# Merging the gated and the forward stage of a spectral convolution kernel, storing its modes once, and fetching the first weights earlier

## The chip, the cores and the metric

The kernel runs on one core of one Trainium2 chip. The metric is the time of one execution on the device in microseconds (us); lower is better. Five engines work side by side: PE (TensorE, matmuls), DVE (VectorE), ACT (ScalarE), POOL (GpSimd) and SP (SyncE, which only issues DMAs here). Each runs its own list of instructions in order, and they wait for each other on semaphores. 16 DMA engines move the data; SP, ACT and POOL each feed them through a queue of their own.

## The reference

`x` is 8 images of 64 channels of 256 x 256 pixels, float32, which is 134 MB. Two layers are computed, and each is added to its own input.

```python
# layer 0: x = x + L0(gn(x))
y   = einsum('bwhc,dc->bwhd', xp, mlp1_w) + mlp1_b      # C -> 3C
x1, x2 = shift1(y[..., :c]), shift2(y[..., c:2*c])      # one pixel in 4 directions
a   = sum(x1) + sum(x2)
bar = softmax(gelu(a @ sa1_w.T) @ sa2_w.T)              # 2 gates per channel
o   = (bar0 * x1 + bar1 * x2) @ mlp2_w.T + mlp2_b
o   = o * sigmoid(batchnorm(x) * wbn) * x
# layer 1: x = x + L1(gn(x))
x_ft = rfft2(x)
top  = einsum('bixy,ioxy->boxy', x_ft[:, :, :32, :32],  w1)   # complex
bot  = einsum('bixy,ioxy->boxy', x_ft[:, :, -32:, :32], w2)
out  = irfft2(top and bot in their corners, zero elsewhere)
```

`gn` is a group norm over pairs of channels. The four weight tensors of layer 1 (real and imaginary part of `w1` and `w2`, 64 x 64 x 32 x 32 each) are 16.8 MB each, 67 MB in all.

## The kernel before

The program has three blocks; at the end of a block all engines meet before the next one starts.

1. **Statistics.** SP loads `x` in tiles of 2 MB, DVE takes mean and variance of each (L288), and ACT adds up the edges that the shifts need.
2. **Gated stage** (layer 0). It has 128 steps, 32 for each pair of images. A step takes 8 rows of a pair: SP loads them (`mix_u`), POOL and ACT make a shifted copy (`mix_v`), PE convolves (L484), DVE gates the result in two passes (L752, then L759, which also adds up the pixels into `sums`), and ACT stores it to the scratch tensor `x_scratch` (L537). The block ends when all 128 stores have landed.
3. **Forward, mode and inverse stage** (layer 1), on one 192 KB area per partition named `arena`.

The **forward stage** reads the 8 images back as 64 tiles of 8 channels (2 MB each, two DMAs of 1 MB on SP's queue, L901). Each tile has 2 halves, so there are 128 halves, numbered `u`, 16 to an image. For each half DVE adds the two image halves (`sums_of`, L1255), POOL subtracts them (L1418), and PE transforms along rows (L985) and transposes (L999). DVE copies the turned blocks to `A` (`turned`, L1275). ACT squares the pixels for the variance (L1125). While an image runs through this, PE transforms the columns of the image before it in 5 parts (L1033), beside which the group norm's scale of that image is made. The scaled modes of a finished image are copied to `XB` by ACT and DVE (L1152, L1310). At `u % 16 == 11` DVE adds the mean to one mode (L1318) and writes the negated imaginary part to a third plane of `XB` (`negate`, L1314). ACT stores the modes to `modes_in` (L1160).

A complex product on real matmuls needs the modes of each image twice: as (real, imaginary) and as (-imaginary, real). Before, both copies are stored, 2 MB for an image, and both are loaded.

The **mode stage** has 8 chunks of 256 modes. A chunk needs 8 MB of weights, issued by POOL (`weights`, L1432, a real and an imaginary DMA of 4 MB), and 2 MB of modes, issued by SP (L920). There are two buffers for each. A chunk is two rounds `r` of matmuls (L1078); after each round ACT and DVE copy half of the result out (L1196, L1368) and ACT stores it to `modes_out`. `mixed` counts rounds. The buffers of chunk `ch` come free when chunk `ch - 2` is done:

```python
for ch in range(2, 2 * NCH):
    pool.wait_ge(mixed, 2 * (ch - 1))
    weights(ch, 0, C)
```

The first weights are issued by POOL behind all forward work, and the modes of the first chunks behind the stores of the last image.

The **inverse stage** turns the modes back into pixels: PE makes rows (L1094) and columns (L1104), DVE adds them to the tile of `x_scratch` (L1402), and POOL stores the tile to `out` (L1448), 2 MB each, 64 tiles in 8 buffers.

The order on each engine is the order of the code; there is no planner. In what follows `fwd_`, `mix_`, `mode_` and `inv_` at the start of a name say to which stage it belongs, and `B * NRF` (256) is the count of all row transforms.

## Time and profile before

| | before |
|---|---|
| median of 3 runs | 2747.92 us (2746.04 to 2749.49) |
| profiled execution, its own time | 2745.33 us |
| its span, first to last instruction | 2743.3 us |
| granted TensorE clock, mean | 0.957 |
| PE busy | 2146.6 us (78%) |
| DVE busy | 2021.8 us (74%) |
| ACT busy | 1404.3 us (51%) |
| POOL busy | 975.5 us (36%) |
| moved by DMA | 957.95 MB, mean 349 GB/s |

By time the stages are: statistics to about 340 us, gated stage to 1250, forward stage to 1810, mode stage to 2086, inverse stage to the end. A busy share is a mean over the whole span; which engine or transfer sets the end differs from stage to stage.

### The profile page before, as it was taken

What the parts mean: (1) busy time and instruction counts of PE and PEld (TensorE: products, weight loads), DVE (VectorE), ACT (ScalarE), POOL (GpSimd) and SP (SyncE); (2) the same over time, 40 slices, a digit from 0 to 9 for tenths busy, and PEclk for the clock granted to TensorE, in tenths of its full rate; (3) what the DMA queues carried; (4) which work ended last, traced back from release to release, by engine and by line L of the source; (5) the groups of instructions that cost most, each with busy time, mean ns of one, the idle gap of its engine ahead of it and who ended that gap; (6) DMA issues with size and microseconds to landing.
All of it is one profiled execution on the core that took longest, in us unless ns stands there. A gap on an engine that the chain in (4) does not pass through costs nothing.

```text
span 2743.3 us, 34783 instructions
## 1 busy us (share of the span) xinstructions
PE 2146.6 (78%) x12978; PEld 1066.9 (39%) x12978; DVE 2021.8 (74%) x2280; ACT 1404.3 (51%) x1757; POOL 975.5 (36%) x555
## 2 busy tenths in 40 slices
PE   0000099999999999996999999956777999888895
PEld 0000033333333333332555555536775555444452
DVE  8999989999999999997888888840003665555453
ACT  1111189888888888885777777720002221221110
POOL 1000035663456556546765656621000222111121
PEclk9999999999999999998999999988888999999997
DMA  9999789999999999988677777779998999999999
GB/s 400 431 431 421 325 273 353 340 342 342 344 340 350 329 344 354 338 278 331 251 272 274 276 274 270 253 261 332 397 400 333 409 417 417 417 417 417 417 417 379
DMA packets 420187, 957.95 MB, mean 349 GB/s; under 512 B 13996, under 2 KB 326108, under 8 KB 375932
## 3 DMA queue, kind: packets, MB, share of 16 engines
q1 hardware_dynamic: 230332, 594.31, 57.7%
q0 software_dynamic: 52208, 201.95, 18.5%
q10 hardware_dynamic: 137488, 159.53, 17.4%
q8 instruction: 104, 1.70, 0.2%
q14 instruction: 55, 0.45, 0.0%
HBM read 662.00 MB, written 293.60 MB: 348 GB/s over the span
## 4 chain that ended last, share of the span: by engine, by line
PE 29%; DMA 16%; DVE 5%; issue 2%; ACT 0%; SPq 0%; POOL 0%; ACTq 0%; DVEq 0%
DMA out<-arena 8%; PE psum L1104 8%; PE psum L985 7%; PE psum L1078 5%; PE psum L1033 4%; DMA arena<-modes_in 4%; PE psum L999 3%; DVE arena L1255 3%; DMA arena<-modes_out 2%; PE psum L1094 2%; DVE arena L1275 1%; DMA arena<-x_scratch 1%; DVE arena L1402 0%; DVE arena L1314 0%; DMA modes_in<-arena 0%
## 5 line engine op out<-in xcount | busy, mean ns | idle before, releaser
L484 PE MATMUL psum<-mix_u,wcur 128*64 128x512 f32 x2048 | 880.0, 592 | 2.1 <-DVE mix_u L588 2.1
L484 PE MATMUL psum<-mix_v,wcur 128*64 128x512 f32 x2048 | 880.0, 592 | 0.0
L1104 PE MATMUL psum<-tab_irow_icol,inv_t 128*128 128x512 f32 x1024 | 491.1, 603 | 48.9 <-ACT inv_t L1226 47.4
L484 PEld LDWEIGHTS psum<-mix_u,wcur 128*64 128x64 f32 x2048 | 278.0, 136 | 589.4 <-issue 581.5
L1402 DVE TENSOR_TENSOR arena<-arena,psum 128x1024 f32<-128x1024 f32 x256 | 312.5, 1221 | 225.6 <-PE psum L1104 220.1
L1418 POOL TENSOR_TENSOR arena<-arena 128x1024 f32<-128x1024 f32 x128 | 349.2, 2736 | 231.5 <-PE psum L985 185.8
L389 POOL COPY mix_v<-mix_u 64x2321 f32<-64x2321 f32 x126 | 383.8, 3046 | 13.8 <-PE psum L484 6.0
L752 DVE SCALAR_TENSOR_TENSOR tiles<-psum,pcur,tiles 128x2048 f32<-128x2048 f32 x128 | 300.6, 2349 | 49.9 <-PE psum L484 49.8
L759 DVE SCALAR_TENSOR_TENSOR tiles<-tiles 128x2048 f32<-128x2048 f32 x128 | 316.9, 2476 | 4.0
L530 ACT ACTIVATE tiles<-tiles,pcur 128x2048 f32<-128x2048 f32 x128 | 268.2, 2095 | 98.1 <-DVE tiles L759 94.3
L1448 POOL DMA_DIRECT2D out<-arena x128 | 115.3, 905 | 562.6 <-DVE arena L1402 562.6
L288 DVE BATCH_NORM_STATS2 stats<-tiles 128x6 f32<-128x512 f32 x512 | 305.3, 675 | 13.2 <-DMA tiles<-x 13.0
L1226 ACT ACTIVATE inv_t<-psum 128x256 f32<-128x256 f32 x256 | 97.5, 384 | 420.1 <-PE psum L1094 420.1
L985 PE MATMUL psum<-arena,tab_frow_fcol_both_ident 128*64 128x512 f32 x1024 | 262.5, 633 | 33.1 <-DVE arena L1255 33.0
L1125 ACT ACTIVATE arena<-arena 128x1024 f32<-128x1024 f32 x256 | 269.8, 1054 | 27.8 <-DMA arena<-x_scratch 25.4
L484 PEld LDWEIGHTS psum<-mix_v,wcur 128*64 128x64 f32 x2048 | 278.0, 136 | 0.0
L498 ACT ACTIVATE mix_v<-mix_u 64x2322 f32<-64x2322 f32 x128 | 273.8, 2139 | 6.1 <-POOL mix_u L380 3.0
L1104 PEld LDWEIGHTS psum<-tab_irow_icol,inv_t 128*128 128x128 f32 x1024 | 197.2, 193 | 191.8 <-issue 128.2
L1255 DVE TENSOR_TENSOR arena<-arena 128x1024 f32<-128x1024 f32 x128 | 254.7, 1991 | 2.8 <-DMA arena<-x_scratch 2.4
L518 ACT ACTIVATE tiles<-mix_u,pcur 128x2048 f32<-128x2048 f32 x128 | 254.5, 1988 | 0.1
L1078 PE MATMUL psum<-arena 128*16 128x64 f32 x4096 | 169.5, 355 | 89.1 <-issue 53.7
L403 PE MATMUL psum<-raw,s_ones_dmask_spread_npix 128*128 128x24 f32 x4 | 1.0, 385 | 297.7 <-PEq L211 297.7
(188 smaller groups left out, 2063.4 us busy)
## 6 DMA issues: line engine op xcount, KB each, us to landing
arena<-x_scratch SPq DMA_DIRECT2D x254, 1024.0 KB, 8.8
mix_u<-x SPq DMA_DIRECT2D x120, 1280.0 KB, 9.5
tiles<-x SPq DMA_DIRECT2D x64, 2048.0 KB, 12.4
x_scratch<-tiles ACTq DMA_DIRECT2D x128, 1024.0 KB, 8.9
out<-arena POOLq DMA_DIRECT2D x128, 1024.0 KB, 42.2
arena<-L_conv_w_real POOLq DMA_DIRECT2D x7, 4096.0 KB, 22.0
arena<-L_conv_w_imag POOLq DMA_DIRECT2D x7, 4096.0 KB, 31.4
arena<-modes_in SPq DMA_DIRECT2D x8, 2048.0 KB, 32.2
```

The source lines that it names most:

```text
L288: last = nc.vector.bn_stats(stats[:, at:at + 6], XT[t % NX][:, q * 512:(q + 1) * 512])
L389: nc.gpsimd.tensor_copy(V[n % NV][C:P, 0:k], U[n % NU][C:P, SHIFT:SHIFT + k]).then_inc(up_done, 1)
L484: last = nc.tensor.matmul(bank(k * 4 + q, 512, C, e * C), wcur[j][:, e, m * C:(m + 1) * C], taps[e][:, r0:r0 + 2, m:m + W], start=(m == 0) ...
L498: nc.scalar.activation(V[n % NV][0:C, 0:k], U[n % NU][C:P, 0:k], ACT.Copy).then_inc(low_done, 1)
L752: nc.vector.scalar_tensor_tensor(out=G[n % 4][:, :], in0=psum[:, k * SC:(k + 1) * SC], scalar=pcur[j][:, 3:4], in1=G[n % 4][:, :], op0=ALU ...
L759: nc.vector.scalar_tensor_tensor(out=G[n % 4][:, :], in0=G[n % 4][:, :], scalar=1.0, in1=XC[n % 4][:, :], op0=ALU.add, op1=ALU.mult, accum ...
L985: last = nc.tensor.matmul(bank(n % 4, 512, C, par * C), frow[:, par, :], ED[n // 2 % NE][par][:, n % 2 * 2:n % 2 * 2 + 2, :], start=True, ...
L1078: last = nc.tensor.matmul(psum[32 * k:32 * k + 2 * B, at:at + C], XM[j][:, :, kx * M2 + ky], WT[j][:, :, kw * M2 + ky], start=True, stop=True)
L1104: last = nc.tensor.matmul(bank(n % 2 * 2 + a), TS[n % 2][:, a * P:(a + 1) * P], icol, start=True, stop=True)
L1255: v.tensor_tensor(ED[h % NE][0][:, :, :], XWF[t % NXF][:, 0, half, :], XWF[t % NXF][:, 1, half, :], ALU.add).then_inc(sums_done, 1)
L1402: nc.vector.tensor_tensor(xw, xw, psum[:, n % 2 * 1024:n % 2 * 1024 + 1024] .rearrange("p (a k) -> p a k", a=2), ALU.add).then_inc(added, 1)
L1418: nc.gpsimd.tensor_tensor(ED[h % NE][1][:, :, :], XWF[t % NXF][:, 0, half, :], XWF[t % NXF][:, 1, half, :], ALU.subtract).then_inc(diff_do ...
```

## The change

- **One block and one area.** The gated and the forward stage stand in one block, so no engine meets the others between them. The gated stage's buffers lie in `arena` too. SP loads the first forward tiles where gated buffers come free: tile 0 after convolution 124 of 128, tile 1 after 127, tile 2 after 128, tile 3 when all stores have landed. The tables of the forward stage are loaded in the first block, those of the inverse stage at the end of the forward loads.
- **POOL makes the first two sums** as well as the first two differences, while DVE gates the last rows. The five small DVE operations on the group means move from ahead of the first sum to `u == 2`. There are 4 buffer pairs for sums and differences, not 3 (`NE`).
- **Modes once.** `XB` has two planes and `modes_in` one copy, 1 MB for an image; `negate` goes, and the signs sit in the table `fcol`. In the mode stage DVE makes the second copy of each chunk (`turn`): a shuffle that swaps neighbouring partitions, and a multiplication by a column of signs (`alt`). The loads of modes move from SP's queue to POOL's, each just ahead of the weights of its chunk.
- **First weights early.** POOL issues 50 of 64 output channels of chunk 0's weights ahead of its last subtraction, the other 14 at the end of the forward rows, and behind them 46 of 64 of chunk 1's. The last image's modes for chunk 0 go straight from `XB` to the chunk's buffer.
- **Inverse.** The first output tile is stored in four pieces, each after its own addition.

```diff
+            KB = 256
+            arena = sb(ph, "arena", [P, 192 * KB])
...
-                    for k in range(4):
-                        sp.wait_ge(stored[k], NI // 4 * 16)
...
                 @block.sync
                 def _(sp):
-                    for n in ("frow", "fcol", "both", "ident"):
-                        sp.dma_start(*TF[n]).then_inc(f_tab, 16)
                     for t in range(B * NG):
                         c, g = t // NG, t % NG * CG
+                        if t < NXF:
+                            sp.wait_ge(conv_done, NI - (4, 1, 0, 0)[t])
+                        if t % (2 * NG) == 0 or t == NXF - 1:
+                            for k in range(4):
+                                sp.wait_ge(x1_stored[k], ((c // 2 + 1) * NB if t != NXF - 1 else NI) // 4 * 16)
...
-                    for ch in range(2 * NCH):
...
-                        sp.dma_start(XM[j][:, :, :], xm[:, :, pos:pos + MC]).then_inc(w_loaded[j], 16)
...
-                    def negate(k0, k1):
-                        nc.vector.tensor_scalar(XB[:, 2, k0:k1, :], XB[:, 1, k0:k1, :], -1.0, None,
-                                                ALU.mult).then_inc(neg_done, 1)
...
+                    v.memset(onecol[:, :], 1.0)
+                    dve.wait_ge(o_done, NI)
+                    v.reduce_sum(sv[:, 0, 0:NQ], sums[:, :].rearrange("p (q n) -> p q n", q=NQ), axis=AX_X).then_inc(n2, 1)
...
+                    dve.wait_ge(sums_done, 2)
                     for u in range(NU_ + 1):
...
+                    def turn(j, b0, b1, n):
+                        to, of = XM[j][:, 2 * b0 + 1:2 * b1:2, :], XM[j][:, 2 * b0:2 * b1:2, :]
+                        v.stream_shuffle(to, of, [lane ^ 1 for lane in range(32)]).then_inc(x_turned, 1)
+                        dve.wait_ge(x_turned, n + 1)
+                        v.tensor_scalar(to, to, alt[:, 0:1], None, ALU.mult).then_inc(x_ready, 1)
+                    dve.wait_ge(x_loaded[0], 16)
+                    turn(0, 0, B - 1, 0)
+                    dve.wait_ge(first_moved, 32)
+                    turn(0, B - 1, B, 1)
                     for r in range(NRO):
...
+                        ch = r // 2 + 1
+                        if h == 0 and ch < 2 * NCH:
+                            dve.wait_ge(x_loaded[ch % 2], (ch // 2 + 1) * 16)
+                            turn(ch % 2, 0, B, ch + 1)
...
                 @block.gpsimd
                 def _(pool):
...
+                    pool.wait_ge(up_done, NI)
+                    pool.wait_ge(conv_done, NI - 3)
                     for h in range(2 * B * NG):
                         t = h // 2
+                        if h == 2 * B * NG - 1:
+                            pool.wait_ge(f_col_done, (B - 1) * PARTS)
...
+                            weights(0, 0, W0_EARLY)
...
+                        if h < 2:
+                            nc.gpsimd.tensor_tensor(ED[h][0][:, :, :], XWF[0][:, 0, half, :], XWF[0][:, 1, half, :],
+                                                    ALU.add).then_inc(sums_done, 1)
...
-                    weights(0, 0, C)
-                    weights(1, 0, C // 2)
-                    pool.wait_ge(modes_stored, B * 48)
-                    weights(1, C // 2, C)
+                    weights(0, W0_EARLY, C)
+                    pool.wait_ge(modes_stored, (B - 1) * 16)
+                    modes(0, B - 1)
+                    weights(1, 0, W1_EARLY)
+                    pool.wait_ge(f_col_done, B * PARTS)
+                    pool.wait_ge(modes_stored, B * 16)
+                    pool.wait_ge(first_moved, 32)
+                    modes(1, B)
+                    weights(1, W1_EARLY, C)
                     for ch in range(2, 2 * NCH):
                         pool.wait_ge(mixed, 2 * (ch - 1))
+                        modes(ch, B)
                         weights(ch, 0, C)
```

DVE between the gated and the forward stage, before. L752 and L759 are the two passes of the last gated step, L1255 the forward sums, L1263 and L1275 copies out of `psum`:

```order
L752 SCALAR_TENSOR_TENSOR tiles<-psum,pcur,tiles 128x2048
L759 SCALAR_TENSOR_TENSOR tiles,sums<-tiles 128x2048
L346 UNCONDITIONAL_BRANCH
L1230 UNCONDITIONAL_BRANCH
L1233 MEMSET fwd_ones 128x1
L1234 TENSOR_REDUCE norm_values<-sums 128x4
L1236 TENSOR_SCALAR norm_values<-norm_values 128x4
L1239 COPY norm_values<-psum 128x4 x2
L1240 TENSOR_SCALAR mrow<-psum 1x512
L1242 TENSOR_TENSOR norm_values<-norm_values 128x8
L1244 TENSOR_SCALAR norm_values<-norm_values 128x8
L1255 TENSOR_TENSOR arena<-arena 128x1024 x3
```

The same place now; L896 and L903 are the gated passes, L1264 the sums:

```order
L896 SCALAR_TENSOR_TENSOR arena<-psum,pcur,arena 128x2048
L903 SCALAR_TENSOR_TENSOR arena,sums<-arena 128x2048
L1254 UNCONDITIONAL_BRANCH
L1332 MEMSET fwd_ones 128x1
L1334 TENSOR_REDUCE norm_values<-sums 128x4
L1336 TENSOR_SCALAR norm_values<-norm_values 128x4
L1264 TENSOR_TENSOR arena<-arena 128x1024
L1272 COPY arena<-psum 128x512
L1284 COPY arena<-psum 128x2x68 x4
```

The block's end is gone, one sum stands where three stood, and the copies and the four groups behind them (L1239 to L1245) stand three sums later.

POOL at the end of the forward stage, before. L1418 is the subtraction, L1432 the weights; chunk 0 is the first 64x64x256 pair:

```order
L1418 TENSOR_TENSOR arena<-arena 128x1024 x128
L1432 DMA arena<-L_conv_w_real 64x64x256
L1432 DMA arena<-L_conv_w_imag 64x64x256
L1432 DMA arena<-L_conv_w_real 64x32x256
L1432 DMA arena<-L_conv_w_imag 64x32x256
```

The same place now; L1471 is the subtraction, L1447 the weights, L1485 the modes:

```order
L1471 TENSOR_TENSOR arena<-arena 128x1024 x126
L1447 DMA arena<-L_conv_w_real 64x50x256
L1447 DMA arena<-L_conv_w_imag 64x50x256
L1471 TENSOR_TENSOR arena<-arena 128x1024
L1447 DMA arena<-L_conv_w_real 64x14x256
L1447 DMA arena<-L_conv_w_imag 64x14x256
L1485 DMA arena<-modes_in 128x7x256
L1447 DMA arena<-L_conv_w_real 64x46x256
L1447 DMA arena<-L_conv_w_imag 64x46x256
L1485 DMA arena<-modes_in 128x8x256
```

Two weight DMAs stand ahead of the last subtraction, and the modes stand in the same queue as the weights.

DVE at the start of the mode stage now (before, the 16 copies L1368 follow each other). L1382 and L1384 are `turn`, L1395 is the copy of a round's result:

```order
L1382 STREAM_SHUFFLE arena<-arena 128x7x256
L1384 TENSOR_SCALAR arena<-arena,tab_frow_fcol_both_ident_alt 128x7x256
L1382 STREAM_SHUFFLE arena<-arena 128x256
L1384 TENSOR_SCALAR arena<-arena,tab_frow_fcol_both_ident_alt 128x256
L1395 COPY arena<-psum 128x1024
L1382 STREAM_SHUFFLE arena<-arena 128x8x256
L1384 TENSOR_SCALAR arena<-arena,tab_frow_fcol_both_ident_alt 128x8x256
```

From here on a shuffle and a multiplication of 2048 elements stand between the two copies of each chunk but the last.

## Rows read from the trace of the kernel before

**Rows 1.** The page's part 2: GB/s moved in 40 equal slices.

```profile
GB/s 400 431 431 421 325 273 353 340 342 342 344 340 350 329 344 354 338 278 331 251 272 274 276 274 270 253 261 332 397 400 333 409 417 417 417 417 417 417 417 379
```

**Rows 2.** The chain that ended last: start us, us, what.

```profile
1824.68 35.39 DMA arena<-modes_in
```

**Rows 3.** Timeline where the gated stage ends: start us, us, engine line op.

```profile
1240.75 0.59 PE L484 MATMUL psum<-mix_u,wcur 128*64 128x512 f32 x1
...
1246.00 0.08 DVE L759 DVE_READ_ACCUMULATOR tiles<-tiles 128x1 f32 x1
...
1250.92 0.29 DVE L1234 TENSOR_REDUCE norm_values<-sums 128x4 f32<-128x128 f32 x1
...
1258.32 0.67 DVE L1240 TENSOR_SCALAR mrow<-psum 1x512 f32<-1x512 f32 x1
...
1261.83 10.01 DVE L1255 TENSOR_TENSOR arena<-arena 128x1024 f32<-128x1024 f32 x3 [2.35 <-DMA arena<-x_scratch]
```

**Rows 4.** Groups of instructions by line, 1325 to 1800 us: busy us, mean ns.

```profile
L1318 DVE TENSOR_TENSOR arena<-arena,ncur 64x1 f32<-64x1 f32 x7 | 16.2, 2321 | 0.0
...
L1314 DVE TENSOR_SCALAR arena<-arena 64x2048 f32<-64x2048 f32 x7 | 8.5, 1208 | 0.0
```

**Rows 5.** Timeline of DVE in the forward stage, two images four apart.

```profile
1515.64 2.32 DVE L1318 TENSOR_TENSOR arena<-arena,ncur 64x1 f32<-64x1 f32 x1
1517.89 1.21 DVE L1314 TENSOR_SCALAR arena<-arena 64x2048 f32<-64x2048 f32 x1
...
1795.58 2.32 DVE L1318 TENSOR_TENSOR arena<-arena,ncur 64x1 f32<-64x1 f32 x1
```

**Rows 6.** Timeline of PE at the same place.

```profile
1522.45 3.56 PE L985 MATMUL psum<-arena,tab_frow_fcol_both_ident 128*64 128x512 f32 x8 [1.55 <-DVE arena L1255]
...
1526.97 1.94 PE L985 MATMUL psum<-arena,tab_frow_fcol_both_ident 128*64 128x512 f32 x8
```

**Rows 7.** Busy time by window there; after POOL: granted clock, DMA share, GB/s.

```profile
1522.40:1526.10 3.70, 3.65 (x9) 0.92 (x10) 2.66 (x7) 1.62 (x4) 0.00 (x0) 0.55 1.01 337
```

**Rows 8.** Timeline of POOL, end of the forward stage and mode stage.

```profile
1795.08 2.80 POOL L1418 TENSOR_TENSOR arena<-arena 128x1024 f32<-128x1024 f32 x1 [0.51 <-PE psum L985]
1809.15 1.71 POOL L1432 DMA_DIRECT2D arena<-L_conv_w_real  x1 [11.27 <-PE psum L999]
...
1881.55 1.82 POOL L1432 DMA_DIRECT2D arena<-L_conv_w_real  x1 [37.92 <-PE psum L1078]
```

**Rows 9.** Timeline of DVE at the end of the forward stage.

```profile
1802.54 1.20 DVE L1255 TENSOR_TENSOR arena<-arena 128x1024 f32<-128x1024 f32 x1
...
1824.12 2.08 DVE L1310 TENSOR_SCALAR arena<-psum,ncur 64x256 f32<-64x256 f32 x5 [5.30 <-PE psum L1033]
```

**Rows 10.** Timeline of PE in the mode stage.

```profile
1860.31 32.41 PE L1078 MATMUL psum<-arena 128*16 128x64 f32 x804 [35.21 <-DMA arena<-modes_in]
...
2060.91 11.92 PE L1078 MATMUL psum<-arena 128*16 128x64 f32 x283 [3.66 <-issue]
...
2079.52 4.16 PE L1078 MATMUL psum<-arena 128*16 128x64 f32 x101 [0.67 <-issue]
```

**Rows 11.** Busy time by window: end of the forward stage, mode stage.

```profile
1785.00:1810.00 25.00, 21.54 (x128) 11.55 (x127) 22.67 (x47) 15.91 (x31) 11.19 (x5) 1.00 0.40 85
...
1920.00:2000.00 80.00, 61.57 (x1468) 58.06 (x1460) 7.92 (x6) 7.08 (x6) 8.17 (x5) 0.90 1.03 397
```

**Rows 12.** The page's part 5 and part 6: a long DVE pass, and the loads of modes.

```profile
L759 DVE SCALAR_TENSOR_TENSOR tiles<-tiles 128x2048 f32<-128x2048 f32 x128 | 316.9, 2476 | 4.0
...
arena<-modes_in SPq DMA_DIRECT2D x8, 2048.0 KB, 32.2
```

**Rows 13.** Busy time by window in the inverse stage.

```profile
2108.00:2114.00 6.00, 6.00 (x18) 3.04 (x17) 3.22 (x4) 1.12 (x3) 1.79 (x2) 1.00 0.52 216
2114.00:2120.00 6.00, 6.00 (x18) 3.23 (x17) 3.77 (x4) 1.12 (x3) 0.21 (x1) 1.00 0.68 264
...
2200.00:2700.00 500.00, 451.63 (x1233) 237.40 (x1232) 273.69 (x233) 98.35 (x226) 91.92 (x103) 0.95 1.02 417
```

480 lines of the change are left out of this document (256 added, 224 removed).

## The prediction, made before the changed kernel was run

> **What bounds the kernel now.** I read the slices of the page first, then the chain of waits, then the timeline at each border between stages. The slices [rows 1] show DMA at 417 GB/s through the inverse stage and 397 to 400 in most of the mode stage, against 251 to 276 in most of the forward stage. So the statistics, the mode stage and the inverse stage are bound by transfers; there only fewer bytes or fewer gaps help. The forward stage has DMA to spare, so work between engines sets it. The reader should look for three holes: none of the engines works between the gated and the forward stage; the last 25 us of the forward stage move 85 GB/s [rows 11]; and the chain shows 35.39 us of PE waiting for the first modes [rows 2, 10].
>
> All moves below are against the profiled execution, 2745.3 us by its own time (its span is 2743.3). The three runs have a median of 2747.9, 2.6 above it, and I add that at the end.
>
> **Border between gated and forward stage.** The last convolution ends at 1241.3, the last gating pass at 1246.1; the first three forward sums end at 1261.83 + 10.01 = 1271.8 [rows 3]. Between lie the last store, the block's end, the tables and the load of the first tile. Now tile 0 is loaded from convolution 124 on (some 7 us a step by the stage times, so 28 us ahead of the end), tile 1 from 127, and POOL has the first two halves done before DVE is free. After 1246.1 DVE does a reduction of 0.29 us [rows 3], one small operation and only the third sum. With POOL working beside it that sum costs up to 10.01 / 3 = 3.3 us, so it ends at about 1250, 22 us sooner. Tile 3 waits for the last store, as the whole stage did before, but it is needed only at half 6; at 3.3 us for a half that is about 1265, and it should land at 1260. Against this stand the five small operations at `u == 2`. Before, POOL stood still while they ran (one took 0.67 us [rows 3]); now it subtracts. An operation on one element took 2.32 us in such a place [rows 4], so it waited for POOL. From below the five cost 1.4 us, with two or three such waits 7; I take 4. The border gives **-18**, between -15 and -21.
>
> Earlier tables in the first stage are 0.5 MB more on a stage that is bound by transfers: at the 431 GB/s of its slices [rows 1] **+1**.
>
> **Forward stage.** An image takes 70 us there ((1795.58 - 1515.64) / 4 [rows 5]). In its first ten halves PE is the last (it also has the columns), in the last six DVE is: at 1515.64 it runs L1318 and L1314 one after the other [rows 5], PE waits and then starts its rows 1.55 us late [rows 6]. `negate` is 7 times 1.21 us [rows 4], all on that path: -8.5. Behind the wait the granted clock falls to 0.55 [rows 7], nearly all at the lower of its two levels, 1.2 GHz, and eight row matmuls take 3.56 us and not 1.94 [rows 6]. What PE did before it fell was to wait twice, some 3.5 us in all. With 1.2 us less of this the clock may stay up, which would give back 1.6 us for each image, 11 in all; it may also not. I take half, -5.5. The fourth buffer pair (`NE`) gives nothing in steady state: POOL is started by a row transform four halves back and not three, at the same moments, and no wait of PE on POOL is among the long ones. That ACT issues one DMA and not three is also worth nothing, since its next copy waits for PE anyway. Forward: **-14**, between 0 and -20.
>
> **Start of the mode stage.** Now PE starts at 1860.3 [rows 10]. What is late next? Weights: POOL issues the first 50 channels before its last subtraction, which started at 1795.1 [rows 8], and that subtraction has slack, since the last sum of DVE ends at 1803.7 [rows 9]; the two issues at 1.7 us each [rows 8] hide in it. The transfers flow from about 1795 into the hole of 85 GB/s. Chunk 0 is 8.4 MB of weights and 0.9 MB of modes: at 397 GB/s [rows 11] 23 us, so 1819 with latency. DVE: its last scaled copies end at 1824.12 + 2.08 = 1826.2 [rows 9], and then come the two turns. No row shows a shuffle. The nearest for 2048 elements at 128 partitions is 2.48 us [rows 12], the lowest conceivable is the 1.21 of [rows 4], and at four times the nearest it would be 10. I take 2.5 for the shuffle and 1.2 for the multiplication: 3.7 for a full chunk, 4.2 with both turns of chunk 0. So PE starts at 1831, and what is last is DVE and no longer a transfer: **-29**, between -22 (shuffle of 10 us) and -31. Chunk 1 needs the last image's modes stored (at 1827 as before, landed near 1837), loaded (1842), turned (1847); PE asks for it at 1831 + 21 = 1852, since chunk 0 took until POOL's issue at 1881.55 [rows 8, 10]. Weights for it are there at about 1849.
>
> The Trainium skill, "VectorE: DVE Perf Modes", section on the perf-mode tier table, gives a shuffle some 2400 ns for 2048 elements and no faster mode; no run here shows it. By it the start would be the same within 0.1 us.
>
> **Chunks 2 to 7.** From the issue at 1881.55 [rows 8] to the landing of chunk 7 at 2060.9 [rows 10] are 179.4 us. In it went 6 chunks of 10.5 MB and 7 MB of results: 70 MB, or 392 GB/s, the rate of the windows. Six times 1.05 MB of modes less is 6.3 MB: -16 us. But POOL's loop gets tighter: a chunk needs 23 us of PE (2060.9 to 2083.7 [rows 10]), a load 26.4, so the next load is asked for only 3.4 us before the queue runs dry, and issuing modes and the first weights takes some 2.7 of them, before the first byte. Gaps of 0 to 2 us a chunk are likely: I take **-12** (bounds -16 and 0). The turn is hidden: the modes of a chunk land 3 to 5 us after the weights of the chunk before, DVE is free about 12 us into the chunk, and the 3.7 us end well ahead of the 23. Tables no longer loaded here: 0.4 MB, **-1**.
>
> The Trainium skill, "SBUF — State Buffer", section on its two separate sides, says that POOL can't write the descriptors of its DMAs while DVE runs an operation that takes both port pairs. By it the multiplications (1.2 us each) could hold back POOL's issues, up to 8 x 1.2 = 10 us in the worst case. In this kernel's order they fall in the middle of a chunk, where POOL has at most its second weight DMA left to issue, so I leave the sum as it is. It is one way in which rival A comes about.
>
> **Inverse stage.** At 417 GB/s [rows 13] it is bound by transfers, and its bytes stay. At its start DMA runs at 0.52 and 0.68 for 12 us [rows 13], waiting for the first whole tile. Storing it in quarters fills 1.5 MB of this: **-3** (0 to -5).
>
> **Sum.** -18 + 1 - 14 - 29 - 12 - 1 - 3 = -76: 2669.3 for a profiled execution, **2672** against the median. Adding up the ends gives -93 and -37, 2655 to 2711 against the median.
>
> **Rivals.**
> A, the chunk period does not fall: the mode stage is held by its loop (issue, load, PE, issue) and not by bytes; then chunks 2 to 7 give 0 and the start perhaps 4 less. For it: one buffer's cycle is load plus PE, and a weight DMA of POOL is issued late in each chunk. Against it: DMA share 1.03 at 397 GB/s [rows 11]. Time: 2672 + 12 + 4 = 2688.
> B, the merged forward stage gives nothing inside itself: POOL and DVE hold each other up as much as before and the clock falls all the same, while the first image pays the full 7 us. Time: 2672 + 14 + 3 = 2689. For it: 2.32 us for one element [rows 4]. Against it: `negate` is plainly on the path.
> C, more than I allow: the clock stays up and DVE's saving counts fully, the tail of the gated stage is shorter, no gaps in the mode stage: 2672 - 6 - 3 - 4 - 2 = 2657.
> D, the early weights don't flow: the two issues stand in POOL's list, but the transfers start only when the forward work is over, at 1809. Then chunk 0 lands at 1835 and PE starts 4 us later: 2676. It is within the forecast's own range.
> E, slower: the turn. PE's chunk waits for `x_ready`, and DVE reaches the turn only in the middle of the chunk before, at 11.5 us, and behind a copy that is no longer than the pass of 2.5 [rows 12]. It decides from 26.4 - 14 = 12.4 us a turn on; with T us, eight chunks cost 7 (T - 12.4) + (T - 3.7), which eats the 76 us at T = 21 and gives 2773 at 24. The rows put T at 3.7, so this would take a shuffle eight times as dear as the nearest pass.
>
> **Chances.** Forecast (with D) 0.58, A 0.14, B 0.12, C 0.13, E 0.03. The forecast's own range is 2660 to 2684; with A, B and C the time is between **2652 and 2696** 8 times in 10. What a measurement here can tell from no change is 0.2%, 5.5 us. All cases but E are faster by far more; I keep 0.01 for no change.
>
> **What would show it right or wrong.** The sums start within 2 us of the last gating pass and the third ends at about 1250; if PE idles over 10 us there, the first term is wrong. Images in the forward stage follow each other at 68 us and not 70; the clock after L1318 tells whether the 1.6 us are in it. Weights flow while the last rows run; PE starts its first mode matmul about 30 us sooner relative to the end of the rows; a shuffle lasts 2.5 us. Chunks 2 to 7 land 26 to 28 us apart and not 29.9 (179.4 / 6). The inverse stage keeps 417 GB/s. The forecast is wrong if a stage that I hold fixed (statistics, gated, inverse) moves by over 5 us, or if PE waits for DVE in the mode stage.

## The result and the profile after

The changed kernel takes 2687.54 us (median of 4 runs, 2679.96 to 2688.57), the kernel before 2746.98 beside it. The ratio is 0.978 [0.976, 0.980]: it is faster, by 59 us. The forecast was 2672 in a range of 2652 to 2696, so that range held the time, and the point was 15.5 us too low. The forecast's own range, 2660 to 2684, did not hold it: only the wider one, with the rivals in it, did. The profiled execution has a span of 2686.7 us at a mean granted clock of 0.969.

The slices of the page after, against [rows 1]:

```profile
GB/s 399 431 430 422 333 266 345 340 347 344 341 340 349 335 343 339 338 348 313 318 258 255 258 263 266 260 281 346 367 382 331 416 416 417 416 418 417 417 417 384
```

The statistics and the inverse stage are where they were. The slices of the mode stage (346, 367, 382) stay below the 397 to 400 of before, though fewer bytes have to move. To see where the 56.6 us between the two profiled spans went, I cut both at the same events:

| from | to | before | after | change | forecast |
|---|---|---|---|---|---|
| start | end of the last gating pass | 1246.1 | 1252.4 | +6.4 | +1 |
| there | image 0's mean added (L1318, now L1323) | 129.5 | 109.4 | -20.1 | -18 |
| there | image 6's mean added | 420.0 | 415.6 | -4.4 | a part of -14 |
| there | last columns start | 14.0 | 11.4 | -2.5 | a part of -14 |
| there | first mode matmul | 50.8 | 20.9 | -29.9 | -29 |
| there | issue of chunk 2 | 21.2 | 23.6 | +2.4 | 0 |
| there | chunk 7 has landed | 179.4 | 173.8 | -5.6 | -12 |
| there | end | 682.4 | 679.5 | -2.9 | -1 - 3 |

**The border.** DVE's timeline after, which answers to [rows 3] (start us, us, engine line op):

```profile
1250.13 2.29 DVE L903 SCALAR_TENSOR_TENSOR arena<-arena 128x2048 f32<-128x2048 f32 x1
...
1252.46 0.29 DVE L1334 TENSOR_REDUCE norm_values<-sums 128x4 f32<-128x128 f32 x1
...
1254.57 1.21 DVE L1264 TENSOR_TENSOR arena<-arena 128x1024 f32<-128x1024 f32 x1
...
1264.28 0.17 DVE L1356 TENSOR_TENSOR norm_values<-norm_values 128x8 f32<-128x8 f32 x1
```

The third sum ends 3.4 us behind the last gating pass, where it was 25.7. Two of those 22 us are lost again a little later. Tile 3 waits for the last store and POOL for tile 3: it landed at 1267.8, 15.4 us behind the last gating pass, and POOL was ready for it 7.9 us behind, where the forecast had 19. The same wait is why the five small operations took only 1.3 us: POOL stood still beside them. POOL's timeline:

```profile
1267.82 54.45 POOL L1471 TENSOR_TENSOR arena<-arena 128x1024 f32<-128x1024 f32 x17 [7.49 <-DMA arena<-x_scratch]
```

**The forward stage.** DVE and PE in image 2, against [rows 5, 6], and the window of PE's slow rows, against [rows 7]:

```profile
1499.51 2.33 DVE L1323 TENSOR_TENSOR arena<-arena,ncur 64x1 f32<-64x1 f32 x1
1501.76 1.10 DVE L1284 COPY arena<-psum 128x136 f32<-128x136 f32 x4
1502.70 2.65 DVE L1264 TENSOR_TENSOR arena<-arena 128x1024 f32<-128x1024 f32 x1
```

```profile
1505.40 3.41 PE L998 MATMUL psum<-arena,frow_fcol_both_ident_alt 128*64 128x512 f32 x8 [1.77 <-DVE arena L1264]
...
1509.76 1.94 PE L998 MATMUL psum<-arena,frow_fcol_both_ident_alt 128*64 128x512 f32 x8
```

```profile
1505.40:1508.80 3.40, 3.40 (x9) 0.83 (x10) 2.61 (x6) 1.38 (x2) 0.00 (x0) 0.56 1.00 354
```

The negation is gone, but the addition of one element still takes 2.33 us, PE still waits 1.77 us behind it, and the granted clock still falls to 0.56 afterwards, most of the way to the lower level of 1.2 GHz. The clock half of the forecast (-5.5) did not come.

**The start of the mode stage.** POOL, DVE and PE, against [rows 8 to 10]:

```profile
1771.10 1.48 POOL L1447 DMA_DIRECT2D arena<-L_conv_w_real  x1
1772.58 1.40 POOL L1447 DMA_DIRECT2D arena<-L_conv_w_imag  x1
1773.99 2.39 POOL L1471 TENSOR_TENSOR arena<-arena 128x1024 f32<-128x1024 f32 x1
...
1833.38 0.91 POOL L1485 DMA_DIRECT2D arena<-modes_in  x1 [16.73 <-PE psum L1093]
```

```profile
1803.39 2.08 DVE L1319 TENSOR_SCALAR arena<-psum,ncur 64x256 f32<-64x256 f32 x5 [5.30 <-PE psum L1046]
...
1805.40 2.12 DVE L1382 STREAM_SHUFFLE arena<-arena 128x1792 f32<-128x1792 f32 x1
1807.56 1.28 DVE L1384 TENSOR_SCALAR arena<-arena,frow_fcol_both_ident_alt 128x1792 f32<-128x1792 f32 x1
...
1878.10 4.37 DVE L1382 STREAM_SHUFFLE arena<-arena 128x2048 f32<-128x2048 f32 x1
```

```profile
1788.81 15.55 PE L1046 MATMUL psum<-frow_fcol_both_ident_alt,arena 128*128 128x128 f32 x136
1809.74 5.56 PE L1093 MATMUL psum<-arena 128*16 128x64 f32 x132 [5.37 <-DVE arena L1384]
...
2007.19 5.13 PE L1093 MATMUL psum<-arena 128*16 128x64 f32 x120 [5.73 <-DMA arena<-L_conv_w_imag]
```

As forecast, the last thing that PE waits for is DVE's turn and no transfer, and the turn of chunk 0 took 4.2 us.

**Chunks 2 to 7.** Busy time by window (after POOL: granted clock, DMA share, GB/s), against [rows 11]:

```profile
1885.00:1890.00 5.00, 3.53 (x89) 3.20 (x81) 1.23 (x1) 1.02 (x1) 1.15 (x2) 1.00 0.86 338
1890.00:1895.00 5.00, 3.28 (x84) 3.26 (x88) 0.00 (x0) 0.00 (x0) 3.17 (x2) 0.66 0.88 238
...
1833.40:2007.20 173.80, 128.08 (x3067) 120.92 (x3057) 51.90 (x31) 15.66 (x13) 25.78 (x18) 0.89 0.98 372
```

At each border between two chunks the rate dips. In the middle of a chunk it does not (406, 405 and 397 GB/s in the three windows from 1900 to 1915). The dips are the gaps that the forecast put at 0 to 2 us a chunk and rival A at all that the bytes save.

### The profile page after: what moved, and what is told of

Same layout as the page of the kernel before. It is cut to its first block, busy times and chain, and to the rows that moved or that the text cites. A ratio compares the mean times of both kernels' runs of the same rounds, so it can differ in the third digit from the quotient of the medians.

```text
span 2686.7 us, 34793 instructions
## 1 busy us (share of the span) xinstructions
PE 2148.0 (80%) x12978; PEld 1220.7 (45%) x12978; DVE 2080.3 (77%) x2296; ACT 1404.0 (52%) x1757; POOL 935.1 (35%) x577
## 4 chain that ended last, share of the span: by engine, by line
PE 49%; DMA 15%; DVE 12%; issue 7%; ACT 3%; POOL 1%; ACTq 0%; SPq 0%; DVEq 0%; POOLq 0%
PE psum L629 21%; DMA out<-arena 8%; PE psum L1119 8%; PE psum L998 7%; PE psum L1046 4%; PE psum L1093 4%; PE psum L1010 3%; DMA arena<-L_conv_w_imag 3%; DVE arena L1264 3%; DVE arena L896 2%; DVE arena L903 2%; DMA arena<-modes_out 2%; PE psum L1109 2%; DVE arena L1284 2%; ACT arena L643 1%
## 5 line engine op out<-in xcount | busy, mean ns | idle before, releaser
L629 PE MATMUL psum<-arena 128*64 128x512 f32 x4096 | 882.7, 592 | 2.2 <-DVE arena L732 1.8
L629 PEld LDWEIGHTS psum<-arena 128*64 128x64 f32 x4096 | 447.0, 136 | 437.7 <-issue 328.9
L1471 POOL TENSOR_TENSOR arena<-arena 128x1024 f32<-128x1024 f32 x128 | 347.9, 2726 | 191.7 <-PE psum L998 177.4
L534 POOL COPY arena<-arena 64x2321 f32<-64x2321 f32 x126 | 349.1, 2771 | 14.8 <-PE psum L629 7.1
L675 ACT ACTIVATE arena<-arena,pcur 128x2048 f32<-128x2048 f32 x128 | 268.1, 2095 | 106.4 <-DVE arena L903 101.8
L903 DVE SCALAR_TENSOR_TENSOR arena<-arena 128x2048 f32<-128x2048 f32 x128 | 319.2, 2494 | 4.0
L896 DVE SCALAR_TENSOR_TENSOR arena<-psum,pcur,arena 128x2048 f32<-128x2048 f32 x128 | 300.5, 2347 | 27.3 <-PE psum L629 26.7
L323 DVE BATCH_NORM_STATS2 arena<-arena 128x6 f32<-128x512 f32 x512 | 305.4, 676 | 14.2 <-DMA arena<-x 14.0
L998 PE MATMUL psum<-arena,frow_fcol_both_ident_alt 128*64 128x512 f32 x1024 | 260.7, 630 | 29.1 <-DVE arena L1264 28.8
L643 ACT ACTIVATE arena<-arena 64x2322 f32<-64x2322 f32 x128 | 273.8, 2139 | 6.1 <-POOL arena L525 3.0
L663 ACT ACTIVATE arena<-arena,pcur 128x2048 f32<-128x2048 f32 x128 | 254.5, 1989 | 0.1
L1264 DVE TENSOR_TENSOR arena<-arena 128x1024 f32<-128x1024 f32 x126 | 249.9, 1983 | 0.4
L732 DVE COPY arena<-arena 64x2321 f32<-64x2321 f32 x128 | 237.8, 1858 | 4.0
```

Of the source, the lines that this page charges most:

```text
L323: last = nc.vector.bn_stats(stats[:, at:at + 6], XT[t % NX][:, q * 512:(q + 1) * 512])
L534: nc.gpsimd.tensor_copy(V[n % NV][C:P, 0:k], U[n % NU][C:P, SHIFT:SHIFT + k]).then_inc(up_done, 1)
L629: last = nc.tensor.matmul(bank(k * 4 + q, 512, C, e * C), wcur[j][:, e, m * C:(m + 1) * C], taps[e][:, r0:r0 + 2, m:m + W], start=(m == 0) ...
L643: nc.scalar.activation(V[n % NV][0:C, 0:k], U[n % NU][C:P, 0:k], ACT.Copy).then_inc(low_done, 1)
L896: nc.vector.scalar_tensor_tensor(out=G[n % 4][:, :], in0=psum[:, k * SC:(k + 1) * SC], scalar=pcur[j][:, 3:4], in1=G[n % 4][:, :], op0=ALU ...
L903: nc.vector.scalar_tensor_tensor(out=G[n % 4][:, :], in0=G[n % 4][:, :], scalar=1.0, in1=XC[n % 4][:, :], op0=ALU.add, op1=ALU.mult, accum ...
```

## The experiments

All ran against the kernel before, with 4 runs each; a ratio is to it, and differences in us are to the changed kernel's 2687.54. Where an experiment touches one place, I read that place's own stretch rather than the total: the same code up to the last gating pass ended between 1247.3 and 1252.4 us in 11 profiled executions, so a total of one run says little about 3 us. (That also belongs to the result: the changed kernel's own +6.4 there is the top of that range; its median is 1249.4, +3.3.) The other stretches vary too where the code is the same: last gating pass to image 0's mean 107.2 to 111.1 us, image 0's mean to image 6's 412.5 to 417.5, issue of chunk 2 to landing of chunk 7 170.4 to 174.7 with a median of 172.0. The experiments ran in three groups, and the medians of the kernel before beside them were 2745.4, 2747.1 and 2747.8, so 2 us of a difference to the changed kernel can come from that alone.

**1. Modes on SP's queue.**

```diff
                     for ch in range(2, 2 * NCH):
                         pool.wait_ge(mixed, 2 * (ch - 1))
-                        modes(ch, B)        # now on SP, behind the same wait
                         weights(ch, 0, C)
```

> The changed kernel, but the modes of chunks 2 to 7 are loaded through SP's queue again (1 MB each, one copy), not through POOL's. Measured so far for the changed kernel: 2687.5 us (4 runs, 2680.0 to 2688.6); from the issue of chunk 2 to the landing of chunk 7 it takes 173.8 us where 163 were forecast, and DMA falls to 238 to 338 GB/s for some 8 us at each chunk border. Theory 1 (POOL's one queue runs dry at each border, since it first issues the modes and only then has weights to issue): the dips go, the stretch falls to 162 to 166 us, time 2677 to 2681. Theory 2 (the loop is held by POOL's second weight DMA, which is issued only when the chunk before has landed): nothing changes, 2686 to 2689.

Measured: 2682.68 us, 0.978 [0.976, 0.980]. The stretch is 171.1 us and not 173.8. That is inside the 170.4 to 174.7 us of kernels whose code is unchanged there, so theory 1 (the issue time of the modes makes the gaps), which wanted 8 to 12 us, gets none that can be told from noise. Chunks land 23 to 33 us apart in turns. POOL's timeline shows it issuing the second half of a chunk's weights late:

```profile
1850.79 1.63 POOL L1453 DMA_DIRECT2D arena<-L_conv_w_real  x1 [17.52 <-PE psum L1099]
1864.54 1.83 POOL L1453 DMA_DIRECT2D arena<-L_conv_w_imag  x1 [12.13 <-issue]
```

**2. The imaginary weights on a queue of their own.** That late issue could be what costs.

```diff
-                        weights(ch, 0, C)                      # real and imaginary on POOL
+                        pool.dma_start(WT[j][0:P:2, :, :], ...).then_inc(p_loaded[j], 16)
...
+                        sp.wait_ge(mixed, 2 * (ch - 1))
+                        sp.dma_start(WT[j][1:P:2, :, :], ...).then_inc(q_loaded[j], 16)
```

> For chunks 2 to 7 the imaginary weights are issued by SP on its own queue, at the same moment as POOL issues modes and real weights on its queue. The changed kernel took 173.8 us from the issue of chunk 2 to the landing of chunk 7. Theory 1 (POOL's queue holds the second 4 MB back until the chunk before has landed, and that makes the dips of the transfer rate at each border): the dips go, the stretch falls to 160 to 166 us, the time to 2672 to 2679 us. Theory 2 (the loop itself: a chunk's load can't be asked for before PE has done the chunk two before, 3 us before the queues run dry): the first bytes come at the same moment as before, at most 1 us sooner a chunk; the stretch stays at 170 to 175 us, the time at 2682 to 2688.

Measured: 2713.46 us, 0.988 [0.986, 0.990]: 26 us slower than the changed kernel, which neither theory had. PE's timeline and the windows of that kernel:

```profile
1873.68 32.79 PE L1101 MATMUL psum<-arena 128*16 128x64 f32 x802 [24.41 <-issue]
...
1940.29 4.96 PE L1101 MATMUL psum<-arena 128*16 128x64 f32 x116 [22.91 <-issue]
```

```profile
1850.00:1870.00 20.00, 0.00 (x0) 0.00 (x0) 0.54 (x1) 0.33 (x1) 2.27 (x2) 0.59 1.04 404
...
1873.00:1895.00 22.00, 21.32 (x528) 21.35 (x532) 7.75 (x5) 1.67 (x2) 0.05 (x1) 0.89 0.62 181
```

PE waits 24 us, then multiplies two chunks in a row (1873.7 to 1917.4), and at the start of that run the transfers fall to 181 GB/s. So chunks 2 and 3 landed together: SP's part of chunk 3 took its share of the rate from chunk 2. Between 1820 and 1960 us SP's parts landed 40.3 us after their issue in the median, POOL's 23.8. From the issue of chunk 2 to the landing of chunk 7 it takes 180.2 us, 6.4 more than in the changed kernel; the larger part of the loss lies behind, where PE has two chunks left and not one. With both parts behind each other on POOL's queue, chunk 2 comes first. What looked like a fault of the queue is what keeps the chunks in order. The Trainium skill, "DMA: Bandwidth & Descriptors", section on queues, rings and completion order, says that each DMA engine goes round its queues packet by packet; by that rule two queues share the rate, and the trace agrees.

**3. Half of the mode matmuls.**

```diff
-                        for ky in range(M2):
+                        for ky in range(0, M2, 2 if 2 <= r < NRO - 2 else 1):
```

> Chunks 1 to 6 compute every second of their mode matmuls only; this part of the result is left out, everything else (loads, turns, copies, stores) stays. PE then needs some 11.5 us a chunk and not 23, so the next load is asked for about 14 us before the queues run dry. Theory 2 (loop of issue, load, PE): the dips at the borders go, and 63.7 MB at 400 GB/s take 159 us: the stretch falls from 173.8 to 157 to 163 us, the time to 2670 to 2676. Theory 1 (POOL's second weight transfer can't be issued while the chunk before is under way): the issue still waits, but the queue has 5 MB ahead of it, so this looks the same in time; it shows in the wait ahead of the issue. Theory 3 (transfers are the bound at some 372 GB/s, whatever is asked for and when): 170 to 175 us, 2682 to 2688.

Measured: 2693.34 us, 0.981 [0.979, 0.983]. Landings of chunks 2 to 6, in PE's timeline:

```profile
1863.24 10.29 PE L1093 MATMUL psum<-arena 128*16 128x64 f32 x256 [23.65 <-DMA arena<-L_conv_w_imag]
1889.24 10.42 PE L1093 MATMUL psum<-arena 128*16 128x64 f32 x256 [15.71 <-DMA arena<-L_conv_w_imag]
...
1968.90 10.24 PE L1093 MATMUL psum<-arena 128*16 128x64 f32 x256 [16.92 <-DMA arena<-L_conv_w_imag]
2009.87 6.59 PE L1093 MATMUL psum<-arena 128*16 128x64 f32 x156 [30.73 <-DMA arena<-L_conv_w_imag]
```

```profile
1864.00:1970.00 106.00, 41.70 (x1040) 39.34 (x1036) 29.69 (x20) 9.17 (x8) 19.36 (x13) 0.71 1.02 404
```

With PE out of the way the dips go (404 GB/s at a share of 1.02), so theory 3 is out, and a chunk takes (1968.90 - 1863.24) / 4 = 26.4 us, against (1978.1 - 1866.2) / 4 = 28.0 in the changed kernel. So 26.4 us is the transfers' own time for a chunk, and the loop of issue, load and PE adds 1.6 us to it. POOL's second issue waits 12.5 to 20.2 us here, and the rate stays up: it is not what makes the dips. Theory 2 holds in its mechanism, and its time does not: the stretch grew to 179.9 us, since chunk 7 took 41.0. The reason is that the first tiles of the inverse stage are asked for as soon as chunk 6 is multiplied, here 13 us sooner, and shared the rate with chunk 7: from 1965 to 2012 us SP's queue moved 8.6 MB and POOL's 9.5. It is the same effect as in experiment 2.

**4. No turn.**

```diff
-                            turn(ch % 2, 0, B, ch + 1)
+                            v.tensor_scalar(XM[ch % 2][:, 1:2, 0:1], ...).then_inc(x_ready, 1)
```

> For chunks 2 to 7 DVE's shuffle and multiplication of 2048 elements are replaced by one multiplication of one element, so the second copy of the modes is left out there; loads and matmuls stay. Theory 2 (loop): DVE's 5.5 to 6 us a chunk are hidden, the stretch stays within 1.5 us of 173.8 and the time within 3 us of 2686. Rival (DVE's passes keep POOL from issuing or slow the copies of results that PE waits for): 1 to 2 us a chunk come back, 162 to 168 us, 2675 to 2680.

Measured: 2687.46 us, 0.978 [0.977, 0.980]; the stretch is 175.5 us. Nothing came back: the 5.5 to 6 us of DVE in each chunk are hidden, and DVE's passes are not what keeps POOL.

**5 and 6. The two halves of the early start.**

```diff
-                            weights(0, 0, W0_EARLY)            # ahead of the last subtraction
...
+                    weights(0, 0, W0_EARLY)                    # behind it
                     weights(0, W0_EARLY, C)
```

> The changed kernel, but POOL issues all of chunk 0's weights behind the forward stage, none ahead of its last subtraction. Theory 1 (the start of the mode stage is bound by DVE at 21 us after the last rows, and the weights alone would be there 4 to 6 us later than that): PE starts its first chunk 4 to 6 us later, time 2691 to 2694. Theory 2 (the early weights carry most of the 30 us gained at this border): PE starts 15 to 20 us later, time 2703 to 2708.

```diff
-                    for r in range(2):
-                        act.dma_start(XM[0][r:P:2, 2 * B - 2, :], ...).then_inc(first_moved, 16)
...
-                    modes(0, B - 1)
+                    modes(0, B)
```

> The changed kernel, but the last image's modes for chunk 0 don't go from XB straight to the chunk's buffer: all of its modes are stored, and chunk 0's modes of all 8 images are loaded when this store has landed. Theory 1 (the detour over memory was the larger part of the wait before): the store lands some 8 us after 1806, the load takes 3 to 6, the turn 4: PE starts 14 to 18 us later and the time is 2701 to 2706. Theory 2 (the early weights were the larger part): PE starts under 6 us later, time 2690 to 2693.

Measured: 2695.15 us, 0.982 [0.981, 0.984], and 2698.59 us, 0.983 [0.982, 0.985]. From the last columns to the first mode matmul:

```profile
1814.22 2.16 PE L1093 MATMUL psum<-arena 128*16 128x64 f32 x46 [19.92 <-DVE arena L1384]
```

```profile
1822.49 7.84 PE L1093 MATMUL psum<-arena 128*16 128x64 f32 x188 [19.73 <-DVE arena L1377]
```

That is 35.5 us (from 1778.74) and 35.3 us (from 1787.20), against 20.9: taking out either half costs this stretch 14.5 us, together 29 of the 29.9. In both PE waits for DVE's turn, and the turn for modes: in the first they stand in POOL's queue behind 8 MB of weights, in the second they go through memory. The totals grew by less, 7.6 and 11.1 us. For the weights a part of that can be seen: image 6's mean comes 68.8 us behind image 5's with the weights late, and 70.4 us in the changed kernel (70.4 to 70.9 in the seven others with early weights and the addition on DVE), where POOL issues them ahead of its last subtraction. So the early issue has a price, some 1.7 us, that the forecast put at nothing. The rest of the difference is spread over stretches that the edit doesn't touch.

**7. The negation put back**, as a multiplication by 1.0 of the same elements.

```diff
                         nc.vector.tensor_tensor(XB[:, 0, 0, 0:1], ...)
+                        nc.vector.tensor_scalar(XB[:, 1, 0:KX, :], XB[:, 1, 0:KX, :], 1.0, None, ALU.mult)
```

> Behind DVE's addition of the mean, in each of the images 0 to 6, a multiplication by 1.0 of the 64 x 2048 imaginary elements is put back where the negation stood; the result is unchanged. Theory 1 (the negation stood on the path between DVE's sums and PE's rows, 1.2 us an image): the forward stage grows by 7 to 9.5 us and the time to 2693 to 2697. Rival (the 6.9 us by which the forward stage got shorter came from the fourth pair of buffers or from other things): it grows by 0 to 3 us, 2686 to 2689.

Measured: 2692.51 us, 0.980 [0.979, 0.982]. Six images (mean of image 0 to mean of image 6) take 421.3 us; the changed kernel takes 415.6, as does the median of its variants with the same code there, and the kernel before took 420.0. So 1.0 us an image, close to the 1.21 that it lasts, is the negation. Put back, it brings the six images to within 1.3 us of the kernel before, which is inside the noise, so nothing can be seen that the fourth pair of buffers or ACT's shorter list gave. The total rose by 5.0 us, just short of theory 1's range.

**8. The first two sums on DVE.**

```diff
-                            nc.gpsimd.tensor_tensor(ED[h][0][:, :, :], ..., ALU.add).then_inc(sums_done, 1)
...
+                    sums_of(0)
+                    sums_of(1)
```

> The first two forward sums are made by DVE behind its last gating pass again, not by POOL; early tiles and the single block stay. Theory 1 (most of the 22 us won at the border come from the single block and the early loads): DVE has two sums of 1.2 to 3.4 us more in front of the third, so the third sum ends 2 to 7 us later after the last gating pass (3.4 us in the changed kernel), and up to 4 us of it come back because POOL no longer works beside DVE's last gating passes; 2686 to 2691 us. Rival (the sums on POOL carry the gain): 10 us or more come back, 2696 us or above.

Measured: 2690.76 us, 0.979 [0.977, 0.982], 3.2 us more, inside theory 1. But its own stretch, last gating pass to image 0's mean, grew by 9.8 us (119.2 against 109.4), at the edge of what the rival asked for. The total hides it because the last gating pass ended at 1247.3, the low end of its range, and not at the changed kernel's 1252.4. The expectation that DVE's last passes would be free of POOL is not borne out: the last of them took 3.45 us and not 2.29 beside POOL's first differences. PE's first rows come 3.4 us behind the last gating pass, where in the changed kernel they come 6.6 us ahead of it; PE's timeline, this kernel and the changed one:

```profile
1250.69 6.45 PE L998 MATMUL psum<-arena,frow_fcol_both_ident_alt 128*64 128x512 f32 x16 [9.28 <-DVE arena L1264]
```

```profile
1245.83 3.62 PE L998 MATMUL psum<-arena,frow_fcol_both_ident_alt 128*64 128x512 f32 x16
```

So POOL's first sums are worth that much where the tiles are early. The five small operations now met a subtraction of POOL:

```profile
1265.02 1.58 DVE L1358 TENSOR_TENSOR norm_values<-norm_values 128x8 f32<-128x8 f32 x1
1266.63 2.28 DVE L1360 TENSOR_SCALAR norm_values<-norm_values 128x8 f32<-128x8 f32 x1
```

**9. Tiles after the last step.**

```diff
                         if t < NXF:
-                            sp.wait_ge(conv_done, NI - (4, 1, 0, 0)[t])
+                            sp.wait_ge(conv_done, NI)
+                        if t == 0: ...                         # and all stores but the last
```

> The loads of the first forward tiles wait for the last convolution and all stores but the last one; the single block and POOL's first sums stay. Theory 1 (the early load is what closes the hole between the stages): the first 2 MB are asked for at about 1248 us and land 7 to 10 us later, POOL's first sum starts there, and PE's first rows come 9 to 14 us later than in the changed kernel; 2696 to 2702 us. Rival (the block's end was the cost, and the loads only follow it): 0 to 4 us, 2686 to 2691 us.

Measured: 2704.08 us, 0.984 [0.983, 0.986], 16.5 us more. PE's first rows come 10.2 us behind the last gating pass and not 6.6 us ahead of it, and image 0's mean 128.7 us behind it, where the kernel before needed 129.5 and the changed one 109.4. PE's timeline:

```profile
1261.20 3.68 PE L1001 MATMUL psum<-arena,frow_fcol_both_ident_alt 128*64 128x512 f32 x8 [14.90 <-issue]
```

So without the early load next to nothing is left of the 20 us of the border: the single block and POOL's first sums are worth little by themselves. The block allows the load, and POOL's sums (experiment 8) are the way in which about half of it is used. It cost 2 us more than theory 1 allowed, since PE's rows came 16.8 us later and not 9 to 14.

**10 and 11. The small operations on ACT.** The 2.33 us for one element, and a copy of 128x128 elements that takes as long, looked like waits for POOL.

```diff
-                        nc.vector.tensor_tensor(XB[:, 0, 0, 0:1], XB[:, 0, 0, 0:1], ncur[0:C, 1:2], ALU.add)
+                        nc.scalar.activation(XB[:, 0, 0, 0:1], XB[:, 0, 0, 0:1], ACT.Identity, bias=ncur[0:C, 1:2])
...
-                        (DVE)  v.tensor_copy(wide_f[...], part[c % 2][...])
+                        (ACT)  nc.scalar.activation(wide_f[...], part[c % 2][...], ACT.Copy)
```

> The changed kernel, but ACT and not DVE makes the two small operations of each image in the forward stage: the mean's addition (2.3 us on DVE) and the spread of the squares (2.4 us on DVE), both of which wait for POOL there. Theory 1 (in the last six of an image's sixteen halves DVE is the last engine, so each microsecond on it is on the path): 7 images times 4.7 us are gained, 33 us, and the granted clock no longer falls once an image; time 2654 to 2664. Theory 2 (POOL's subtractions are as late as DVE there): at most a third of it, 2677 to 2684.

> Of the two small DVE operations that an image has in the forward stage, ACT now makes the addition of the mean to 64 x 1 elements; the copy of 128 x 128 elements (2.39 us each on DVE) stays on DVE. With both on ACT the time was 39.5 us less than the changed kernel's. Theory 1 (each costs what it lasts on DVE, 2.0 to 2.4 us, with the clock falling behind each): the addition alone gives 17 to 22 us, 2665 to 2670 us. Theory 2 (only the addition stands where DVE is the last engine; the copy stands where PE has the columns as well): it gives 30 us or more, 2657 us or less. Theory 3 (the copy carries it): 10 us or less, 2677 us or more.

Measured: 2648.06 us, 0.965 [0.963, 0.967], with both on ACT, 39.5 us less than the changed kernel and better than theory 1 had it; 2670.06 us, 0.972 [0.971, 0.974], with the addition alone, 17.5 us less, which is theory 1's (2665 to 2670) to within 0.1 us. The copy is worth the other 22. Groups by line in the forward stage of the changed kernel, and of the one with both on ACT (busy us, mean ns):

```profile
L1292 DVE COPY fwd_wide<-fwd_part 128x128 f32<-128x128 f32 x6 | 14.3, 2390 | 0.0
L1323 DVE TENSOR_TENSOR arena<-arena,ncur 64x1 f32<-64x1 f32 x7 | 14.1, 2012 | 0.0
```

```profile
L1193 ACT ACTIVATE arena<-arena,ncur 64x1 f32<-64x1 f32 x7 | 2.0, 285 | 0.0
...
L1186 ACT ACTIVATE fwd_wide<-fwd_part 128x128 f32<-128x128 f32 x6 | 1.8, 292 | 0.0
```

And the forward windows of both, changed kernel first:

```profile
1360.00:1780.00 420.00, 387.00 (x2392) 228.44 (x2389) 365.12 (x628) 309.41 (x592) 253.69 (x99) 0.97 0.69 254
```

```profile
1320.00:1740.00 420.00, 409.34 (x2616) 248.15 (x2614) 375.34 (x668) 337.93 (x655) 302.88 (x108) 1.00 0.73 271
```

PE works 409 of 420 us and the clock stays at its upper level. In the changed kernel seven copies of 2.39 us and six additions of 2.33 met POOL's subtractions: 30.7 us. (Those behind POOL's last subtraction take 0.14 to 0.20 us.) An image takes 63.4 us and not 69.3, which is 5.9 for operations of 4.7. The rest is the clock, whose mean rose from 0.97 to 1.00 between the two windows. Experiment 11 prices it: with the addition gone and the copy left, images take 65.7 and 67.4 us in turns, and only in the longer ones do eight row matmuls take 3.6 us and not 1.94. PE's timeline there:

```profile
1443.37 3.56 PE L998 MATMUL psum<-arena,frow_fcol_both_ident_alt 128*64 128x512 f32 x8 [1.45 <-DVE arena L1274]
```

So one fall of the clock costs an image 1.7 us, which is what the forecast put on it (1.6).

**12. Both edits together** (1 and 10).

> Both edits together: the two small operations of each image on ACT, and the modes of chunks 2 to 7 issued on SP's queue. They lie in different stages. Theory 1 (they add up; 2648 with the first alone, and 3 to 5 us of the mode stage for the second): 2643 to 2646 us. Rival (the 3 us of the second are within what one run differs from the next): 2646 to 2651 us.

Measured: 2648.33 us, 0.964 [0.962, 0.965]. They do not add up; the 5 us of experiment 1 do not come back, as the rival had it, and this version is no faster than the one of experiment 10.

## Why the prediction was right and where it was wrong

**Right: the start of the mode stage** (-29 forecast, -29.9 measured), which is half of the gain. The shuffle, bounded from 1.2 to 10 us for lack of a row and taken at 2.5, was 2.12 us with 1792 elements, both turns of chunk 0 took 4.2 as in the sum, and DVE became the last as forecast. Experiments 5 and 6 show that both parts are needed for it. Rival D is out: the early weights flow (253 GB/s in the last 25 us, 85 before).

```profile
1765.00:1790.00 25.00, 22.14 (x134) 12.30 (x133) 21.58 (x49) 16.19 (x31) 11.96 (x7) 1.00 0.67 253
```

**Right: the border and the negation.** -20.1 for -18 (no negation lies in this stretch); and 1.0 us an image for 1.21. Experiments 8, 9 and 7 name the causes. The closeness of the border is in part luck: the 4 us put down for the five small operations were 1.3, for a reason that was not foreseen (POOL waited for tile 3), and that wait cost about what the operations did not. Rival E never came near: the turn is hidden (experiment 4), though at 5 to 6 us in the middle of a chunk it costs more than the 3.7 that the forecast took.

**Wrong: half of the clock's recovery (-5.5).** The step said that with 1.2 us less of waiting "the clock may stay up". It still fell. The cause was in the row that the forecast itself used [rows 4]: the 2.32 us of an operation on one element stayed. Its price was right (1.6 forecast, 1.7 in experiment 11), what it hangs on was not: without this operation the clock falls in every second image only (experiment 11), and without the copy of the squares too it stays up (experiment 10). Rival B was right in this half and wrong in the other.

**Wrong in size: chunks 2 to 7 (-12).** The fewer bytes are real: a chunk of 10.5 MB takes 26.4 us when nothing else holds it (experiment 3). The step took the gaps at 0 to 2 us a chunk and chose the low end, 4 of 16 us in all; they are 1.6 us a chunk between landings, and the stretch gave 5.6 us (7.4 by the median of the kernels with the same code there). By the forecast's own sign the chunks should have come 26 to 28 us apart; they came 29.0 (173.8 / 6). Chunk 0 gave back another 2.4. Its matmuls now run beside more transfers (DMA share 0.99 in its second quarter, where it was 0.76 before), with stops of about 1 us after some 128 matmuls that the trace puts down to issue. For chunks 2 to 7 this is rival A's mechanism, and with chunk 0 it comes to a little over half of A's price (8.8 of 16 us). What causes these stops was not tried. That the measured time falls on A's 2688 is chance: the rest of the distance comes from the clock and the gated stage.

**Not foreseen: the end of the gated stage.** The step held it fixed but for 1 us of tables. It came 6.4 us later in the profiled run, 3.3 in the median of its variants. The first suspect is POOL's forward work beside DVE's last passes: a gating pass took 4.33 us and not 2.29.

```profile
1238.89 4.33 DVE L903 SCALAR_TENSOR_TENSOR arena<-arena 128x2048 f32<-128x2048 f32 x1
```

```profile
1237.52 3.56 POOL L1471 TENSOR_TENSOR arena<-arena 128x1024 f32<-128x1024 f32 x1
```

(DVE's and POOL's timelines; a subtraction alone takes POOL 2.4 us.) But that is not where the 6.4 us are. The 120th of the 128 gating passes already ended 5.7 us late, and POOL's first forward sum starts only at 1227.2. DVE's timeline, before and after:

```profile
1192.46 0.08 DVE L759 DVE_READ_ACCUMULATOR tiles<-tiles 128x1 f32 x1
```

```profile
1198.18 0.08 DVE L903 DVE_READ_ACCUMULATOR arena<-arena 128x1 f32 x1
```

From there to the end of the last pass it is 54.2 us, and 53.5 in the kernel before. In experiment 9, with no forward work beside them, each of the last passes lasted 2.29 us and the stage ended at 1251.0 all the same. Of the 5.7 us, 2.1 are there at the first gating pass (the tables, forecast at 1); what makes the rest was not tried and stays open.

The last two terms, tables and first output tile (-1 and -3), gave 2.9 together, and no experiment separates them. Of the 19.4 us between the forecast for a profiled execution and this one, 5.4 are here, 5.0 in the forward stage and its border, 1.5 around chunk 0, 6.4 in chunks 2 to 7 and 1.1 behind them.

## What to carry to other kernels

Read the mean duration of the tiniest operations: an addition of one element in each partition at 2.3 us was a wait for another engine here, and moving it and one small copy elsewhere gave 39.5 us, two thirds of what the whole change gave. A double-buffered stream whose PE time is close to its load time gets only a part of what fewer bytes promise, and its parts should stay in one queue in the order of their use, because a second queue takes its rate from the chunk that is needed first. Compare variants by stretches between the same events, since stages that an edit doesn't touch moved by up to 5 us from run to run, and before one engine is blamed for the late end of a stage, look how late the stage was before that engine began.

## What the runs showed of the hardware

- **A small operation of DVE can last as long as one of POOL's.** The same addition to 64x1 elements takes 2.33 us while POOL subtracts and 0.14 us when POOL has made its last subtraction; on ACT it takes 0.29. DVE's timeline in image 0 and image 6:

```profile
1361.82 2.33 DVE L1323 TENSOR_TENSOR arena<-arena,ncur 64x1 f32<-64x1 f32 x1
...
1777.39 0.14 DVE L1323 TENSOR_TENSOR arena<-arena,ncur 64x1 f32<-64x1 f32 x1
```

  The Trainium skill, "SBUF — State Buffer", section on its two separate sides, calls the port pair of the two an exclusive lock held for a whole instruction; by that rule a short operation pays the rest of POOL's 2.4 us, and the trace agrees.
- **A shuffle has no fixed price.** 2.12 us for 1792 elements while PE waited, 4.37 us for 2048 in the middle of a chunk. In the seven turns of 2048 elements it took 3.69 to 4.50 us. Transfers ran at 406 GB/s beside the fast one and 412 beside the slow one shown, so they are not the difference; PE's matmuls are, or something that comes with them, and no run tells which. The forecast used 2.5. The Trainium skill, "VectorE: DVE Perf Modes", section on the perf-mode tier table, gives some 2400 ns for 2048 elements: that is near the first, at 2.12 x 2048 / 1792 = 2.42 us, and not the second.
